# Decoder layer in split fp32: the rows of three batches turned in 32 by 32 blocks by VectorE and moved by DMA instead of turned by TensorE

## What is computed

```python
x = _layernorm(x + _L0_attn_ref(x, Wq, Wk, Wv, Wo))         # 16 heads of 64, causal
x = _layernorm(x + _L0_xattn_ref(x, ctx_4096))              # softmax(x ctx^T) ctx, no projections
x = _layernorm(x + _L0_ffn_ref(x, weight, bias, lora_A, lora_B, starts))
# _L0_ffn_ref: y = x @ weight.T + bias, and (x A^T) B^T of the batch's adapter where it has one
```

## Time and profile before

| | us |
|---|---|
| median of three runs | 523.44 |
| the profiled execution | 522.58 |
| its span, first to last instruction | 520.6 |
| TensorE busy | 513.0 |
| VectorE busy | 319.8 |
| ScalarE busy | 262.6 |
| GpSimd busy | 152.1 |

### The profile page before, as it was taken

One profiled execution on the slowest core, in us unless ns is written; L12 is line 12 of the kernel. 1 busy time (PEld: TensorE's weight loads), 2 busy tenths in 40 slices (PEclk: granted clock), 3 DMA queues, 4 the chain that ended last, 5 costly groups with the idle time before them and its releaser, 6 DMA issues.

```text
span 520.6 us, 7823 instructions
## 1 busy us (share of the span) xinstructions
PE 513.0 (99%) x2864; PEld 438.4 (84%) x2864; DVE 319.8 (61%) x693; ACT 262.6 (50%) x664; POOL 152.1 (29%) x139
## 2 busy tenths in 40 slices
PE   8999999999999999999999999999999999999995
PEld 5888888888989888888978888888887888988884
DVE  5822000187776868677674797769887776845432
ACT  5713210183856648384565356357868464525231
POOL 0003500536353554742006150113937000110010
PEclk9999999999999999999999999999999999999998
DMA  8907612331021111100095677579987477333011
GB/s 284 320 16 180 184 40 82 126 118 51 32 69 55 42 40 43 42 2 0 1 280 162 146 205 210 148 200 262 263 247 212 133 207 214 104 91 110 1 75 47
DMA packets 37958, 65.60 MB, mean 126 GB/s; under 512 B 4872, under 2 KB 20616, under 8 KB 37920
## 3 DMA queue, kind: packets, MB, share of 16 engines
q1 hardware_dynamic: 37248, 64.58, 43.1%
q10 hardware_dynamic: 672, 0.52, 0.3%
HBM read 54.08 MB, written 3.67 MB: 111 GB/s over the span
## 4 chain that ended last, share of the span: by engine, by line
PE 98%; DMA 1%; ACT 0%; DVE 0%; SPq 0%; issue 0%; ACTq 0%
PE bank L539 30%; PE bank L656 30%; PE bank L550 15%; PE bank L742 6%; PE bank L566 3%; PE bank L581 3%; PE bank L773 2%; PE bank L775 2%; PE bank L778 2%; PE bank L726 1%; PE bank L715 1%; DMA x_raw<-x_feat 1%; PE bank L687 1%; PE bank L793 1%; PE bank L689 1%; PE bank L796 1%
## 5 line engine op out<-in xcount | busy, mean ns | idle before, releaser
L539 PE MATMUL bank<-x_hi,w_hi 128*128 128x512 f32 (+1 forms) x256 | 93.7, 366 | 0.0
L539 PE MATMUL bank<-x_hi,w_lo 128*128 128x512 f32 (+1 forms) x256 | 93.2, 364 | 0.0
L539 PE MATMUL bank<-x_lo,w_hi 128*128 128x512 f32 (+1 forms) x256 | 93.1, 364 | 0.0
L1386 DVE STREAM_TRANSPOSE prob_t<-prob 32x256 f32<-32x256 f32 x160 | 69.7, 436 | 12.1 <-ACT prob L947 9.4
L656 PE MATMUL bank<-wo,act_hi 128*128 128x512 f32 x224 | 70.2, 395 | 0.0
L656 PE MATMUL bank<-ffn,act_hi 128*128 128x512 f32 x224 | 70.0, 394 | 0.0
L1755 POOL TENSOR_TENSOR w_lo<-w_mix,w_hi 128x1024 fp32r<-128x1024 f32 x16 | 38.3, 2396 | 104.6 <-ACT w_hi L922 104.6
L937 ACT ACTIVATE prob<-prob,shift 112x112 f32<-112x112 f32 x128 | 47.8, 378 | 40.8 <-DVE shift L1369 40.8
L1768 POOL TENSOR_TENSOR norm<-norm,minus_half 128x1 f32<-128x1 f32 (+1 forms) x22 | 16.8, 765 | 156.5 <-DVE norm L1459 156.5
L539 PEld LDWEIGHTS bank<-x_hi,w_hi 128*128 128x128 f32 x256 | 48.1, 188 | 6.0
L539 PEld LDWEIGHTS bank<-x_lo,w_hi 128*128 128x128 f32 x256 | 48.1, 188 | 5.1
(11 more groups left out here) (119 smaller groups left out, 960.6 us busy)
## 6 DMA issues: line engine op xcount, KB each, us to landing
cf_raw<-ctx_feat SPq DMA_DIRECT2D x32, 376.0 KB, 4.1
ct_raw<-ctx_tok SPq DMA_DIRECT2D x24, 448.0 KB
w_raw<-qkv_w SPq DMA_DIRECT2D x16, 512.0 KB, 3.4
half_raw<-wo_w SPq DMA_DIRECT2D x16, 256.0 KB, 5.8
half_raw<-ffn_w SPq DMA_DIRECT2D x16, 256.0 KB, 7.0
wv_raw<-qkv_w SPq DMA_DIRECT2D x15, 256.0 KB, 7.2
x_raw<-x_feat SPq DMA_DIRECT2D x7, 448.0 KB, 8.1
out<-y_t SPq DMA_DIRECT2D x6, 512.0 KB, 3.9
```

The costliest lines, as they stand in the source:

```text
L539: last = pe.matmul(to[:, 0:cols.stop - cols.start], a[:, k, :], b[:, k, cols], start=(k == 0 and b is x_hi and a is w_hi[w]), stop=(k == K ...
L1386: return dve.transpose(quads(prob_t_wide[r], key, query), quads(prob_wide[r], query, key))
```

## The change

For batches 1, 3 and 5 TensorE doesn't turn x2. Instead, as soon as `norm_x2(b)` has written the row buffer, VectorE transposes it in place in blocks of 32 by 32 (`swap_blocks`, one instruction on 128 x 1024). Each block is then turned in itself but still in its old place, and 16 DMAs (`move_blocks`, eight calls with two each) carry the blocks to their place in `act_raw`, which is the memory of `act_lo`: each takes 32 partitions x 8 feature blocks x 32 tokens (16 tokens in the last quarter of the 112). They stand on SyncE's queue. ScalarE rounds the result from SBUF (`round_blocks`), VectorE takes the rest in place (`rest_blocks`). The row buffers now have 128 partitions; GpSimd clears their last 32 once (`rows_set`). `ffn(b - 1, n)` waits for `block_rest`.

The lists of all engines but TensorE are written in another order around this; on SyncE the weight pieces 0 to 15 go out earlier than before. Semaphores are freed by letting the second set of value weights share two (a rounding now waits for four loads).

```diff
-TURNS = ["a0", "a1", "a2", "b0", "a3", "b1", "a4", "b2", "a5", "b3", "a6", "b4", "b5", "b6", "b7"]
+TURNS = ["a0", "a1", "a2", "b0", "a3", "a4", "b2", "a5", "a6", "b4", "b6", "b7"]
+BLOCKS = [1, 3, 5]
+        act_raw = at("act_raw", [P, KT, B * S], A0 + 28672)
-        row = [at(f"row{i}", [S, D], (Q0 + 24576, S0 + 12288, S0 + 16384)[i]) for i in range(ROWS)]
+        row_all = [at(f"row{i}", [P, D], (Q0 + 24576, S0 + 12288, S0 + 16384)[i]) for i in range(ROWS)]
+        row = [r[0:S, :] for r in row_all]
             def copy_row(b, which):
                 if b >= ROWS:
-                    sp.wait_ge(turned, 2 * AT_TURN[f"b{b - ROWS}"] + 2)
+                    if b - ROWS in BLOCKS:
+                        sp.wait_ge(moved, 256 * blocks_before(b - ROWS) + 256)
+                    else:
+                        sp.wait_ge(turned, 2 * AT_TURN[f"b{b - ROWS}"] + 2)
...
+            def move_blocks(b, h):
+                sp.wait_ge(swapped, blocks_before(b) + 1)
+                if blocks_before(b):
+                    sp.wait_ge(moved, 256 * blocks_before(b))
+                q = h // 2
+                t, n = b * S + QUAD * q, min(QUAD, S - QUAD * q)
+                for d in range(2 * (h % 2), 2 * (h % 2) + 2):
+                    sp.dma_start(act_raw[QUAD * d:QUAD * d + QUAD, :, t:t + n],
+                                 row_all[b % ROWS][QUAD * q:QUAD * q + QUAD, :].rearrange(
+                                     "p (k d i) -> p k d i", k=KT, d=QUADS)[:, :, d, 0:n]
+                                 ).then_inc(moved, 16)
...
+            sp.wait_ge(rows_set, ROWS)
             copy_row(0, 0)
...
             def ffn(i, n, turns=0):
-                pe.wait_ge(turn_rest, 2 * AT_TURN[f"b{i + 1}"] + 2)
+                if i + 1 in BLOCKS:
+                    pe.wait_ge(block_rest, 2 * blocks_before(i + 1) + 2)
+                else:
+                    pe.wait_ge(turn_rest, 2 * AT_TURN[f"b{i + 1}"] + 2)
...
             cross_score(3, first)
-            turn_row(1)
             wo(5, 1)
...
             cross_score(5, first)
-            turn_row(3)
             ffn(0, 1)
...
             cross_score(7, first)
-            turn_row(5)
             ffn(2, 1)
...
             def round_wv(c, k):
-                act.wait_ge(wv_in[c][k], 16)
+                if c == 0:
+                    act.wait_ge(wv_in[0][k], 16)
+                else:
+                    act.wait_ge(wv_in[1][k // 4], 64)
...
+            def round_blocks(b):
+                act.wait_ge(moved, 256 * blocks_before(b) + 256)
+                for c in range(2):
+                    ks = slice(4 * c, 4 * c + 4)
+                    act.activation(act_hi[:, ks, tokens_of(b)], act_raw[:, ks, tokens_of(b)],
+                                   ACT.Copy).then_inc(block_rounded, 1)
...
+            def swap_blocks(b):
+                dve.wait_ge(x2_ready, b + 1)
+                dve.transpose(row_all[b % ROWS][:, :], row_all[b % ROWS][:, :]).then_inc(swapped, 1)
+            def rest_blocks(b):
+                for c in range(2):
+                    ks = slice(4 * c, 4 * c + 4)
+                    dve.wait_ge(block_rounded, 2 * blocks_before(b) + c + 1)
+                    dve.tensor_tensor(act_lo[:, ks, tokens_of(b)], act_raw[:, ks, tokens_of(b)],
+                                      act_hi[:, ks, tokens_of(b)].bitcast(F32),
+                                      ALU.subtract).then_inc(block_rest, 1)
...
+            pool.wait_ge(heads_done, 2 * PAIRS)
+            pool.wait_ge(wo_rest, 2 * NB)
+            for i in range(ROWS):
+                pool.memset(row_all[i][P - QUAD:P, :], 0.0).then_inc(rows_set, 1)
+                pool.wait_ge(rows_set, i + 1)
             power(0, 0, P)
```

More of the change, by code:

```diff
@@ L243, in build @@
         x_rounded, x_rest = sem("x_rounded"), sem("x_rest")
-        wv_in = [[sem(f"wv_in{c}_{k}") for k in range(KT)] for c in range(2)]
+        wv_in = [[sem(f"wv_in0_{k}") for k in range(KT)], [sem(f"wv_in1_{h}") for h in range(2)]]
         wv_rounded, wv_rest = sem("wv_rounded"), sem("wv_rest")
@@ L270, in build @@
         turned, turn_rounded, turn_rest = sem("turned"), sem("turn_rounded"), sem("turn_rest")
+        rows_set = sem("rows_set")
+        swapped, moved = sem("swapped"), sem("moved")
+        block_rounded, block_rest = sem("block_rounded"), sem("block_rest")
         cf_in = [sem(f"cf_in{i}") for i in range(4)]
@@ L474, in _ @@
             load_ff(7)
-            copy_row(4, 1)
+            load_cf(15)
+            load_cf(16)
+            move_blocks(1, 0)
+            move_blocks(1, 1)
+            move_blocks(1, 2)
+            move_blocks(1, 3)
+            move_blocks(1, 4)
+            move_blocks(1, 5)
+            load_cf(17)
+            move_blocks(1, 6)
             load_cf(18)
+            move_blocks(1, 7)
             load_ct(3, 0)
@@ L505, in _ @@
             load_ct(5, 2)
+            copy_row(6, 0)
+            copy_row(6, 1)
             store_y(0)
@@ L1153, in _ @@
             cross_exp(2)
+            round_ff(0)
+            round_turned("a3")
             round_cf(14)
-            round_turned("a3")
+            round_ff(1)
+            round_ff(2)
+            round_ff(3)
             round_ct(12)
@@ L1162, in _ @@
             round_ct(16)
-            round_ff(0)
-            round_ff(1)
-            round_turned("b1")
+            round_ff(4)
+            round_ff(5)
+            round_ff(6)
+            round_ff(7)
             round_cf(15)
             norm_x1(4)
-            round_ff(2)
-            round_ff(3)
             round_cf(16)
-            round_ff(4)
+            round_ct(17)
+            cross_exp(3)
+            norm_x1(5)
             round_cf(17)
-            round_ct(17)
-            round_ff(5)
-            cross_exp(3)
-            round_ff(6)
-            round_ff(7)
-            norm_x1(5)
             round_turned("a4")
             round_cf(18)
+            round_blocks(1)
             round_ct(18)
+            norm_x2(2)
             round_ct(19)
-            norm_x2(2)
             keep_cprob_t(3)
@@ L1250, in _ @@
             keep_y(3, 0)
-            round_turned("b5")
             round_cf(31)
@@ L1256, in _ @@
             norm_y(2)
+            round_blocks(5)
             round_ct(42)
@@ L1681, in _ @@
             rest_cf(26)
+            rest_blocks(3)
             rest_ct(30)
@@ L1813, in _ @@
             power(0, 3, P)
-            power(1, 1, S)
             add_one(0)
@@ L1817, in _ @@
             rest_ff(0)
[L1818 to L1819 removed]
             add_one(2)
             add_one(3)
+            rest_ff(1)
+            power(1, 1, S)
             rest_ff(2)
@@ L1824, in _ @@
             rest_ff(4)
-            power(0, 5, P)
+            power(0, 4, P)
             rest_ff(5)
@@ L1828, in _ @@
             rest_ff(7)
+            power(0, 5, P)
             power(1, 2, S)
```

147 lines of the change are left out of this document (81 added, 66 removed).

## The result

The changed kernel takes 526.64 us (median of 8 runs, 524.97 to 527.53), the kernel before, timed beside it, 523.25 us (8 runs): a ratio of **1.0061 [1.0047, 1.0076]**, slower by 0.6%. The forecast was 521.4 us, 0.4% faster. The profiled execution took 527.53 us, span 525.5 us, against 520.6 us before.

What follows compares the result with a forecast made beforehand. TensorE was taken as the bound: 2.35 us removed less a 0.3 us stall gave -2.05 us, so 520.5 us profiled; adding 0.86 us for timed runs gave 521.4 us, range 520.8 to 523.8.

Steps and rivals of the forecast that it cites:

- What bounds the kernel: Whole kernel: TensorE, busy 513.0 of 520.6 us, is the bound as long as operands arrive in time.
- what is removed: TensorE, batches 1, 3 and 5: three turn_row calls and 0.08 us per following block go, 2.35 us in all.
- What is added elsewhere: VectorE swaps at 1.3 us each, rests and roundings that replace others, GpSimd memsets at most 7.2 us; taken as covered.
- a sign against this: Start of the first layer norm: norm_x1(0) starting later than 299.5 us would show the GpSimd cover wrong.
- The moves: SyncE's queue: 16 moves per batch at 0.65 us, 10.4 us in all; the queue, not the DMA engines, sets the pace.
- Rivals B and C: Row moves: B, over about 0.9 us each, about 526 us, 0.13; C, small pieces cost more, 523 to 526 us, 0.07.
- Step (1), chunk 15: Batch 1, last context chunk before 366.56 us: lands late behind eight weight loads, stall 0 to 1.2 us, 0.3 taken.
- Step (2): Batch 1, chunks 17 and 18 behind the first moves: chunk 17 issued at 368.3 us, both covered by over 4 us.
- rival D: Changed order of roundings leaves one operand late, chunk 19 (1.1 us cover) named next: 522 to 523.5 us, chance 0.10.
- The sum: Whole kernel: -2.35 + 0.3 = -2.05 us, giving 521.4 us, 0.4% faster.
- Step (3): Batch 1, ScalarE: round_blocks(1) waits for all 16 moves, yet norm_x2(2) meets 381.5 us; no wait added.
- Batches 3 and 5: Later moves: batch 3 covered by more than 8 us, batch 5 by 1.1 us at VectorE; no loss.

Runs made afterwards that it cites:

- one_move_mended: All three rows swapped, old order up to 400 us, row 1 moved by one DMA instead of sixteen (results wrong), against the kernel before: 521.43 us, ratio 0.9968.
- rows35_tpart: rows35 with ScalarE keeping the low-rank part of tiles 0 and 1 ahead of ct rounding 25, as before the change: 521.56 us, ratio 0.9975.
- moves_only_row1: rows35_tpart with keep_t_part(0) also ahead of ct rounding 24, plus sixteen unused moves of row 1 and row 4's copies displaced: 527.61 us, ratio 1.0078.
- row1_on_tensor: Changed kernel's order, but TensorE turns row 1 again and its sixteen moves are gone; rows 3 and 5 still moved: 523.45 us, ratio 1.0000.
- one_move_row1: Changed kernel with row 1 moved by one DMA of the whole row instead of sixteen (results wrong): 523.51 us, ratio 1.0013.
- rows35: Old order up to about 400 us with row 1 on TensorE, then the changed kernel's order with rows 3 and 5 moved: 523.20 us, ratio 0.9998.
- two_mended: Changed kernel with ct rounding 23 ahead of weight rounding 12 and keep_t_part(0) ahead of ct rounding 25 on ScalarE: 526.33 us, ratio 1.0064.
- three_mended: two_mended with chunk 19's load, rounding and rest also put further ahead: 526.91 us, ratio 1.0085.
- ct23_ahead: Changed kernel with one ScalarE operation moved, ct rounding 23 ahead of weight rounding 12: 526.43 us, ratio 1.0066.
- rows135_interleaved: All three rows swapped and moved, old order up to 400 us, row 1's sixteen moves two by two between loads: 525.84 us, ratio 1.0054.

## Why the prediction was wrong, step by step

*What bounds the kernel*, and *what is removed*: right. TensorE was the bound, and a kernel with cheap moves gains. The 2.35 us was never measured alone: one_move_mended gains 1.7 us (interval 1.1 to 2.3) with 1.0 us of waits left; rows 3 and 5 gave 1.33 of 1.56 in the profile and 1.3 (0.6 to 2.0) in rows35_tpart.

*What is added elsewhere*: right in size. Swap 1.245 us (1.3 taken, from the earlier trace rows), rests 0.62, memsets 2.96 us in all, within the cover of the earlier trace rows. norm_x1(0) starts at 300.38, which the text had named as a sign against this; but before it started at 299.50, and 0.80 of the 0.88 us is the late start.

*The moves*: right in price, 0.61 us each (0.65 taken; 0.66 each for the twelve in a row) and 2.0 us to land; the queue sets the pace. Rivals B and C, which needed over 1 us a move, are out. In moves_only_row1 the engines carry little but moves from 366 to 371 us: a share of 0.37 of 16 engines over 5 us for 56 GB/s is about 13 ns per 128 bytes, an estimate from that row (8 to 32 were bounded). The sums of the whole executions agree roughly: the page's dynamic queue shows 44.2% for 43.1% of the engines' time, with 13,056 packets more, some 10 ns a packet, but profiles with the same packets scatter from 44.0 to 45.1%. So pieces of 128 bytes between two places in SBUF did not take their engine longer than the 32 ns that the larger pieces of the earlier trace rows took. That is what the Trainium skill says in "DMA: Bandwidth & Descriptors", section "Why small descriptors are slow (HBM only)"; a price for the read-modify-write of its section "Specifications" doesn't show here.

*Step (1), chunk 15*: a stall of 0 to 1.2 us forecast, 1.00 measured, for another reason than the one given. The chunk had landed in time (ScalarE rounds it at 365.89 without a wait); VectorE was late and came to the chunk's rest at 367.47, with three ct rests in 2.52 us ahead of it. "VectorE's own queue gets there at about 365.5" was the error. The swap came later than assumed (361.05 to 362.30, where its end was put at 360.5), but it isn't the cause by itself: row1_on_tensor has no swap here and begins the same rest at 367.10, behind three ct rests in 2.99 us. The size was right by luck.

*Step (2)*: chunk 17 was issued at 370.26 (368.3 forecast) and chunks 17 and 18 were never waited for. Right in the changed kernel. But the list of deadlines **ended there, and this is the step that failed**. Behind all sixteen moves stood the context rows of batch 3 and chunk 19; of these the first had no deadline in the sum at all, and chunk 19 only 1.1 us of cover, named in rival D. Measured: the context rows went out 1.9 us later than without the moves, the rounding of chunk 19 began 2.7 us later, and TensorE stood for 1.62 us. The text had the facts in hand: 10.4 us of queue, and DMA engines fully busy from 361 to 378 us. A queue that issues 32 KB in 0.61 us feeds them at some 54 GB/s, an estimate that the 56 GB/s of moves_only_row1 bear out. Every load behind the moves had to be given a new time of issue, and the chain of landings and roundings behind it followed to TensorE; that was done for two chunks and not for the rest.

The sum also put **the new order at nothing**: the only price in it was 0.3 us for chunk 15. The runs show some 1.3 to 1.6 us for it (row1_on_tensor keeps nothing of what rows 3 and 5 bring), in the waits for chunk 15, for piece 23 and for t_both.

*Step (3)*: right. round_blocks(1) waits for nothing, norm_x2(2) ends at 381.06 (deadline 381.5).

*Batches 3 and 5*: right, no wait of TensorE behind 405 us. The moves fall where the engines have room: with the change their share is 0.33 from 405 to 420 us and 0.51 from 450 to 465, so the moves are free there.

*Rival D* had the mechanism and the place (chunk 19, 0.10), and was too small by a factor of two to three: it asked for one late operand. There were three, a fourth hidden behind them (t_both), and the clock. The order alone cost about what the two moved rows brought (row1_on_tensor, 1.000), the moves of row 1 another 2.5 to 3.1 us (one_move_row1 against the changed kernel).

*Not in the prediction at all*: that a stall of TensorE costs more than its length, in some executions; and that VectorE's rests take up to 1.1 us longer where GpSimd takes rests at the same time.

What stays open: whether some order exists in which row 1's sixteen moves pay. Five reordered kernels did not find one. Also open is whether another queue would have room for the moves; no run issues them from any other engine.

## What to carry to other kernels

Price a DMA on a shared queue twice: by its own time, and by what it does to every load behind it. A load that could have gone at once goes later by the whole time of the small transfers (chunk 17 in moves_only_row1, 7.3 us); one that must wait for its place anyway, only by what runs over that wait (the context rows of batch 3, 1.9 us); and where the engines have room, as at batches 3 and 5, it costs nothing. To find the cause of a gap in the transfers, compare with a kernel of the same order without the small ones, not with the kernel before. And when a change reorders a tuned schedule, take every operation that has moved behind a wait (here keep_t_part(0) and a norm behind one landing, worth 2 us alone) through the whole list, since a stall hides the next one: mending the largest wait may bring nothing while others are left. The best version here moves rows 3 and 5 only and keeps the old order around row 1: 521.56 us, against 523 before and 526.6 with the change.

## What the runs showed of the hardware

- A wait of TensorE is sometimes followed by a stretch at 1.2 GHz: here three microseconds at a granted 0.50 behind waits of 1.62 and 1.84 us, 1.14 us lost. The profiles of rows35, two_mended and three_mended show two to three such microseconds behind waits of 2.15, 2.53 and 3.14 us; those of ct23_ahead (2.46), rows135_interleaved (2.69) and moves_only_row1 (3.01) show none. So the length of the wait alone doesn't decide; when it comes was not settled.
- VectorE's rest of a piece of 125 x 512, both inputs in SBUF, has a median of 0.68 us and took up to 1.81 (one_move_row1, 48 of them). The long one in the changed kernel began at 396.28, in the same moment as a weight rest of GpSimd.
- A move of 32 partitions x 8 pieces of 128 bytes within SBUF takes 0.61 us of SyncE's queue (median of 48) and lands 2.0 us after its issue. Twelve in a row took 7.89 us.
- The first 10 us vary by up to 1.0 us from one execution to the next. In the profile of the changed kernel the first seven matmuls take 3.13 us, while seven later ones take 1.75; the granted clock is shown as 1.00 for both.
